# A two-layer cross-attention block on one core: the softmax maximum joined across key quarters on VectorE instead of TensorE, with edits to the seams between stages, the division and the opening

## What is computed

```python
# x (8, 56, 256), ctx (8, 1500, 256); H = 16 heads, K = 128, F = 1024; two layers, one MLP
def _cross_attention(q_in, kv_in, wq, bq, wk, bk, wv, bv, wo, bo, bias_k, bias_v):
    qh = (q_in @ wq + bq).reshape(b, q_len, H, K)
    kh = (kv_in @ wk + bk).reshape(b, t, H, K)
    vh = (kv_in @ wv + bv).reshape(b, t, H, K)
    kh, vh = concatenate([kh, bias_k]), concatenate([vh, bias_v])      # one extra key
    weights = softmax(einsum('bqhk,bthk->bhqt', qh, kh) / sqrt(K))
    return einsum('bhqt,bthk->bqhk', weights, vh).reshape(b, q_len, H * K) @ wo + bo
...
x = x + _cross_attention(layer_norm(x), ctx, ...)      # twice
return x + gelu(layer_norm(x) @ w_fc1 + b_fc1) @ w_fc2 + b_fc2
```

## Time and profile before

| | us |
|---|---|
| median of 3 runs | 1236.87 (1236.75 to 1239.4) |
| the profiled execution's own time | 1234.94 |
| its span, first to last instruction | 1233.1 |
| PE busy | 1210.1, 98% |
| PE weight load busy | 1111.1, 90% |
| POOL busy | 894.0, 72% |
| DVE busy | 833.2, 68% |
| ACT busy | 767.9, 62% |
| DMA | 68 GB/s on average |

### The profile page before, as it was taken

How to read it: one execution, slowest core, us unless ns; L and a number is a source line. 1 busy time by engine, 2 the same in 40 slices (tenths; PEclk the granted TensorE clock), 3 DMA queues, 4 the chain that set the end, 5 groups by cost and what they waited for, 6 DMA issues and landing times. The chain is left out here.

```text
span 1233.1 us, 26572 instructions
## 1 busy us (share of the span) xinstructions
PE 1210.1 (98%) x7736; PEld 1111.1 (90%) x7736; DVE 833.2 (68%) x1395; ACT 767.9 (62%) x1495; POOL 894.0 (72%) x744
## 2 busy tenths in 40 slices
PE   7999999999999999999999999999999999999998
PEld 6779999999999999998896999999999999999897
DVE  6765767676767676676755666676766666677654
ACT  5746666565666565676484656666666666667655
POOL 5737777777777787679551768686868686867882
PEclk9999999999999999999999999999999999999999
DMA  5401222222222222223320122222222222312231
GB/s 179 126 19 51 56 76 55 74 57 73 61 69 64 67 68 61 59 62 102 103 69 18 38 56 71 61 73 58 74 57 74 58 76 56 79 42 65 73 93 38
DMA packets 147720, 83.60 MB, mean 68 GB/s; under 512 B 121116, under 2 KB 122540, under 8 KB 147672
## 3 DMA queue, kind: packets, MB, share of 16 engines
q1 hardware_dynamic: 147128, 82.27, 25.5%
q10 hardware_dynamic: 544, 0.75, 0.2%
HBM read 68.56 MB, written 0.53 MB: 56 GB/s over the span
## 5 line engine op out<-in xcount | busy, mean ns | idle before, releaser
L607 POOL TENSOR_TENSOR pt<-slots,pt 125x512 fp32r<-125x512 f32 (+3 forms) x384 | 451.0, 1181 | 174.9 <-ACT slots L1069 167.6
L782 PE MATMUL psum<-qs,ctx 128*125 128x384 f32 (+1 forms) x2304 | 537.9, 370 | 3.0 <-ACT slots L1095 2.3
L782 PEld LDWEIGHTS psum<-qs,ctx 128*125 128x125 f32 x2304 | 394.2, 186 | 50.3 <-ACT slots L1095 10.1
L799 PE MATMUL psum<-ctx,pt 125*128 125x258 f32 (+1 forms) x1344 | 382.8, 285 | 1.4 <-ACT on L1076 0.5
L800 PE MATMUL psum<-ctx,pt 125*128 125x256 f32 (+1 forms) x1344 | 379.4, 282 | 0.0
L801 PE MATMUL psum<-ctx,pt 125*128 125x258 f32 (+1 forms) x1344 | 378.9, 282 | 0.0
L1068 ACT ACTIVATE pt<-slots 125x512 fp32r<-125x512 f32 (+3 forms) x384 | 221.3, 576 | 232.9 <-DVE slots L1356 221.9
L1368 DVE TENSOR_TENSOR t_max<-psum,t_max 125x512 f32<-125x512 f32 (+1 forms) x320 | 199.0, 622 | 200.9 <-PE psum L782 200.8
L1095 ACT ACTIVATE slots<-psum 125x512 f32<-125x512 f32 (+1 forms) x384 | 206.5, 538 | 121.7 <-DVE t_max L1368 112.6
L799 PEld LDWEIGHTS psum<-ctx,pt 125*128 125x128 f32 (+1 forms) x1344 | 253.5, 189 | 16.1 <-ACT on L1076 3.5
L800 PEld LDWEIGHTS psum<-ctx,pt 125*128 125x128 f32 (+1 forms) x1344 | 254.2, 189 | 6.7
(11 more groups left out here) (105 smaller groups left out, 972.4 us busy)
## 6 DMA issues: line engine op xcount, KB each, us to landing
nat_stage<-ctx_nat SPq DMA_DIRECT2D x60, 375.0 KB
tr_stage<-ctx_tr SPq DMA_DIRECT2D x60, 375.0 KB, 3.1
w_raw<-weights SPq DMA_DIRECT2D x70, 256.0 KB, 2.7
qt<-turn SPq DMA_DIRECT2D x256, 32.0 KB, 2.0
qt<-turn SPq DMA_DIRECT2D x224, 24.0 KB, 1.9
dk_rest<-dk_rows SPq DMA_DIRECT2D x2, 768.0 KB, 5.7
w_raw<-weights ACTq DMA_DIRECT2D x2, 256.0 KB, 4.6
dk_first<-dk_rows SPq DMA_DIRECT2D x2, 256.0 KB, 4.7
```

The source lines that it names most:

```text
L607: nc.gpsimd.tensor_tensor(split_weights(h, LO, c), logits(h, c), as_f32(split_weights(h, HI, c)), ALU.subtract).then_inc(pt_lo, 1)
L782: last = mm(scores(h, k), ctx_tr_chunk(half, a, c), qs[h][:, m, half, 0:R], start=(half, a, m) == terms[0], stop=(half, a, m) == terms[-1])
L799: mm(out_bank[:, 0:D + 2], hi, ctx_nat_hi(c), start=(c == 0), stop=False, skip_group_check=True)
```

## The change

1. Maximum. PE's two transposes and their waits go. DVE copies the quarters 1 to 3 of `mx_part` (32 partitions by 16 or 12 numbers) beside quarter 0, right after `turned_max`; in the next step it reduces the four (32 partitions, 64 or 48 numbers), and copies the result to partitions 32, 64 and 96. `spread_max` then reads SBUF instead of PSUM.
2. Division. ACT starts on `rden_ready` instead of `pn_ready`. The scaled tiles are two columns wider, and `pn_extra` is copied out of them later (`extra_weights`, before `turn_context`, and once at the end of a layer).
3. Seams. In `norm` the rows 1 and 3 go to ACT (`norm_rows`), rows 0 and 2 stay on DVE; one more short operation makes ACT's bias. ACT's copies of the rows to `xres` come after `norm`. The fourth key-bias product of the next layer moves into the wait for POOL's power. The mask goes on `dv80` (80x128) instead of `p80` (80x448), four buffers deep, and the first heads' mask products no longer wait for `p80`. The MLP's first two blocks use the interleaved order of the first queries.
4. Opening. `hdiff` comes after the statistics, the key-bias products of heads 0 and 1 after the first two `query_lo`, the fourth weight's high part into the query loop. Throughout the query loop a weight's high part is made one head later in ACT's order, before the copies of the carried queries.
5. `NAT_STEPS` 13 becomes 14 (DVE and POOL).

```diff
-NAT_STEPS = (9, 13, 17, 21)
+NAT_STEPS = (9, 14, 17, 21)
@@ POOL, output stage
+                def mask_values(h, u):
+                    nc.gpsimd.tensor_tensor(dvm[u][:], as_f32(dv80[:]), mask[:, ds(h, 1)].to_broadcast([EXTRA, K]),
+                                            ALU.mult).then_inc(dvm_ready, 1)
+                weight_lo(l * JOBS + H, 0)
+                for u in range(4):
+                    mask_values(u, u)
+                weight_lo(l * JOBS + (H + 1), 1)
...
                 with pool.Fori(0, QUADS - 1) as quad:
                     for u in range(4):
                         weight_lo(l * JOBS + quad * 4 + (H + 4 + u), u)
-                        mask_extra(quad * 4 + (u + 4), u % 2, l * H + quad * 4 + (u + 3))
+                        pool.wait_ge(c_mm, INIT + l * H + quad * 4 + (u + 1))
+                        mask_values(quad * 4 + (u + 4), u)
@@ PE, first_contexts
-                for u in range(2):
-                    pe.wait_ge(pm_ready, INIT + n + u + 1)
-                    mm(C_BANK[u][:, 0:ROWS], dv80[:], pm[u][:], start=False, stop=True).then_inc(c_mm, 1)
+                    pe.wait_ge(dvm_ready, INIT + n + u + 1)
+                    if u == 0:
+                        pe.wait_ge(p80_lo, INIT + n // H + 1)
+                    mm(C_BANK[u][:, 0:ROWS], dvm[u][:], p80[:], start=False, stop=True).then_inc(c_mm, 1)
@@ PE, batch_steps
-                        if c == 0 and (h == 1 or not first) and k < NCT + (0 if tail else 1):
-                            pe.wait_ge(mt_reduced, INIT + group)
-                            max_by_block(1 - h)
-                        if c == 1 and (h == 1 or not first) and k < NCT + (0 if tail else 2):
-                            pe.wait_ge(max_ready, INIT + group)
-                            max_by_query(1 - h)
@@ ACT
+            def norm_rows(m):
+                act.wait_ge(ln_chain, INIT + m * LN_CHAIN + LN_CHAIN)
+                for g in range(1, RG, 2):
+                    go(xn[:, g, :], Y_BANK[g][0:RGP, 0:D] if m else xres[:, g, :], ACT.Identity,
+                       bias=ln_b[:, g:g + 1], scale=ln_r[:, g:g + 1]).then_inc(xn_act, 1)
...
-                    act.wait_ge(pn_ready, INIT + l * GROUPS + b * 2 + (h + 1))
+                    act.wait_ge(rden_ready, INIT + l * GROUPS + b * 2 + (h + 1))
@@ DVE
+                def gathered_max(b, h):
+                    dve.wait_ge(mt_reduced, INIT + group + 1)
+                    for a in range(1, BLOCKS):
+                        V.tensor_copy(mx_part[0:BLOCK, a, 0:n], mx_part[a * BLOCK:(a + 1) * BLOCK, 0, 0:n]).then_inc(mt_gathered, 1)
                 def group_max(b, h):
-                    dve.wait_ge(mt_mm, INIT + group + 1)
-                    V.tensor_reduce(mx_group[0:n].rearrange("p (a q) -> p a q", a=BLOCKS), ...
+                    dve.wait_ge(mt_gathered, INIT + (group + 1) * (BLOCKS - 1))
+                    V.tensor_reduce(mx_all[0:BLOCK, 0:n], mx_part[0:BLOCK, :, 0:n].rearrange("p a j -> p j a"),
+                                    X, ALU.max).then_inc(max_ready, 1)
+                    dve.wait_ge(max_ready, INIT + group + 1)
+                    for a in range(1, BLOCKS):
+                        V.tensor_copy(mx_all[a * BLOCK:(a + 1) * BLOCK, 0:n], mx_all[0:BLOCK, 0:n]).then_inc(max_spread, 1)
...
-                    V.tensor_tensor(pn_extra[:, at], sums[:, D + 1], rden[:, at], ALU.mult).then_inc(pn_ready, 1)
+                def extra_weights(b, h):
+                    dve.wait_ge(on_act, INIT + l * (2 * GROUPS) + b * 4 + (2 * h + 2))
+                    dve.wait_ge(on_dve, INIT + l * (3 * B) + b * 3 + (2 + h))
+                    V.tensor_copy(pn_extra[:, tiles_of(batch_at(l, b), h)], on[:, 0:GT[h], D + 1]).then_inc(pn_ready, 1)
@@ DVE, batch_steps
                         if c == 1 and ended:
                             group_max(*ended)
                         if (i >= 0 or not first) and not (tail and i >= 0):
                             shifted(b, i, ph, pc)
                         if c >= 1 and not tail:
                             chunk_max(b, k, h, c)
                         if c == 0 and ended:
                             turned_max(*ended)
+                            gathered_max(*ended)
                         if c == 1 and ended:
                             spread_max(*ended)
```

More of the change, by code:

```diff
@@ L171, in build @@
         cs = [sb(f"cs{u}", [P, 2, ROWS], F32R) for u in range(4)]
-        pm = [sb(f"pm{s}", [EXTRA, ROWS], F32R) for s in range(2)]
+        dvm = [sb(f"dvm{u}", [EXTRA, K], F32R) for u in range(4)]
         dv80 = sb("dv80", [EXTRA, K], F32R)
@@ L655, in _ @@
                 pool.wait_ge(dv80_step, INIT + l * 2 + 2)
-                for u in range(2):
-                    weight_lo(l * JOBS + (H + u), u)
[L658 to L675, removed]
+                def mask_values(h, u):
+                    nc.gpsimd.tensor_tensor(dvm[u][:], as_f32(dv80[:]), mask[:, ds(h, 1)].to_broadcast([EXTRA, K]),
+                                            ALU.mult).then_inc(dvm_ready, 1)
+                pool.wait_ge(consts_in, 16 * N_CONSTS)
+                weight_lo(l * JOBS + H, 0)
+                for u in range(4):
+                    mask_values(u, u)
+                weight_lo(l * JOBS + (H + 1), 1)
+                pool.wait_ge(oth_lo, INIT + l * H + 2)
+                for u in range(2, 4):
+                    weight_lo(l * JOBS + (H + u), u)
                 with pool.Fori(0, QUADS - 1) as quad:
@@ L730, in first_queries @@
                         if c == DC - 1:
-                            last.then_inc(q_mm, 1)
+                            last.then_inc(done, 1)
             def residual(m):
@@ L987, in _ @@
                 keep_busy(4)
-            for u in range(2):
-                head_context(u, LAYERS * H + u, LAYERS * JOBS + u, False)
+            pe.wait_ge(c_lo, INIT + LAYERS * H - 2)
+            first_blocks(LAYERS, LAYERS * JOBS, C_BANK, c_mm)
             output_quad(LAYERS * H, LAYERS * JOBS, False, True, False)
@@ L1020, in _ @@
             go(act_ready[:], filler[:, 0:1], ACT.Copy)
-            for u in range(4):
+            for u in range(3):
                 act.wait_ge(w_in[u], 16)
@@ L1319, in query_quad @@
                             tr_part_hi(quad, quad)
-                if l == 0:
-                    dve.wait_ge(dk_first_in, 16)
-                    for u in range(2):
-                        key_bias_product(l, u, u, 0, True)
                 query_lo(0, 0)
@@ L1327, in _ @@
                 if l == 0:
-                    for u in range(2, 4):
+                    dve.wait_ge(dk_first_in, 16)
+                    for u in range(4):
                         key_bias_product(l, u, u, 0, True)
@@ L1469, in _ @@
                 normalized(B - 1, 1, O_LAST)
+                extra_weights(B - 1, 1)
                 dve.wait_ge(ot_mm, INIT + (l + 1) * 2)
```

109 lines of the change are left out of this document (56 added, 53 removed).

## The result

The changed kernel takes 1247.51 us (median of 5 runs, 1244.44 to 1247.82), the kernel before beside it 1236.87 (5 runs): a ratio of 1.0074, with a 95% interval of 1.0061 to 1.0087. The forecast was 1222.5.

What follows compares the result with a forecast made beforehand. PE's own order was taken to bound the attention loop. Loop -4.1, partial entries -2.0, attention's end -2.8, clock -1.7, seam -1.7, third norm -0.3, masks -0.5, opening -1.2: sum -14.3, so 1222.5 us, range 1206 to 1232.

Steps and rivals of the forecast that it cites:

- Copies blocked by POOL: The maximum's DVE copies within SBUF wait for a running POOL instruction: 0.15 us each unhindered, up to 1.3 blocked.
- The pair at k = 0: Transposes in steps 1 and 2 of an entry: removing them wins 0.42 us per entry.
- a race won: At k = 12, third copy against POOL's L558: won, net 0 per entry; lost, 0.45 us more; +0.22 taken.
- Part 5: `NAT_STEPS` 13 to 14 moves L1235's 0.94 us on DVE out of crowded k = 13; no term of its own.
- The division: ACT starts earlier on the scaled tiles: -0.24 us at k = 5, +0.15 at k = 17, per entry.
- First and emptying entries: Four partial entries, first and emptying of each layer: -1 us per layer, -2.0 in all.
- End of attention: First mask product no longer waits for POOL's mask: 1.4 us earlier per layer, -2.8 in all.
- Clock and output stages: Half-speed clock behind attention's end, layer 2 only: -1.7 us; shorter masks on POOL in the output stage: -0.5.
- Seam of the layers: Between layers, fourth key-bias product and its reduce moved away: 0.9 us; norm rows split between engines: 0.8; together -1.7.
- The opening: PE's 1.37 us wait for `qh` goes and the norm is earlier, but the first weight buffer is freed later: -1.2 us.
- rival (c): In the loop, spreading copies each meet one more POOL instruction: 2.3 us per entry, time 1254; chance 0.09.
- Rival (a): In the loop, the maximum's copies are not blocked: an entry wins 1.31 us, time 1208; chance 0.22.

Runs made afterwards that it cites:

- reductions and 13: Changed kernel with the six copies of each group written as maxima over an axis of one element and `NAT_STEPS` back at 13: 1213.38 us.
- experiment 1: `NAT_STEPS` step moved alone: changed kernel with 13 again, 1230.24 us; kernel before with 14, 1246.99 us.
- experiment 3: Both with 13: kernel before with the maximum joined by DVE's copies, 1243.15 us; changed kernel with the transposes on PE, 1225.92 us.
- experiment 5: On reductions and 13: `hdiff` and products back, `pn_extra` copy as a reduction, 1211.41 us; POOL's order at attention's end changed on top, 1211.00.
- experiment 4: Opening edits undone in changed kernel: 1247.01 us; `hdiff` or products alone put back in reductions and 13: 1212.38, 1213.81; opening edits alone on kernel before: 1238.00.
- part 1 alone: Kernel before with only the maximum joined by DVE's copies, no transposes on PE, `NAT_STEPS` with 13: 1243.15 us, ratio 1.0043.

## Why the prediction was wrong, step by step

- **What bounds the kernel: right.** What an entry gained or lost is PE's waits and the two pairs of transposes, and the step bases read from the earlier trace rows held: with reductions and 13 an entry is nothing but these.
- **Copies blocked by POOL: right,** and the schedule of k = 12 to 0.1 us. The pair at k = 0 won 0.39 of its 0.42 (2.84 + 2.87 for the earlier trace rows's 6.10). Steps 12 to 15 grew by 0.21 in the changed kernel, for 0.22 forecast, and that this agrees is luck: 0.22 was the middle between a race won (0) and a race lost (0.45). The race was won in all 12 middle entries (3.27 or 3.28 us each), and 0.13 at step 14 and 0.1 at step 15 were lost even so.
- **Part 5, `NAT_STEPS`, counted at nothing: this is the step that failed.** The prediction moved L1235's 0.94 us on DVE and stopped there. Behind the cast hang POOL's low part, a load on SP's queue, and DVE's own wait for it three steps later. It is +0.69 per entry by itself (experiment 1) and +1.15 in the changed kernel: 16 us, the whole distance from gain to loss. All it needed was to follow one piece round in the trace of before: cast, low part, issue, landing. There the round took 8.2 us and DVE waited 0.20 at its end; over the whole kernel with 13 it waited for that transfer only 6.9 us, but 19 times and up to 0.6: there was hardly any slack to give away.
- **The same number had hidden the cost of the copies.** With the cast at k = 13 the copies cost 0.42 per entry (experiment 3), where the two pairs were to win 0.20: DVE's cast then stands behind the blocked copies and steps 14 to 16 wait. The sum of the pairs holds only for the kernel with 14.
- **The division: mis-sized on the safe side.** k = 5 won 0.22 to 0.25 in layer 1 and 0.27 to 0.30 in layer 2 (0.24 forecast). At k = 17 the step is 2.49 in every kernel with the changed division but those with the copies and 14 together, a gain of 0.14 and not a loss of 0.15; with these it was 2.66, a loss of 0.03.
- **First and emptying entries: -2.0 forecast, +2.2 measured.** Emptying takes 24.59 and 24.58 for 24.04 and 24.06. In the changed kernel it is 24.0 with the transposes and 23.7 with reductions: leaving the transposes out is worth 0.3 and not 1, and the blocked copies cost 0.9. The first entries gained nothing, and in about half the layers they lost 1.0 to 1.2 (last section).
- **End of attention: -2.8 forecast, -1.2 measured.** POOL is out of the product's way, as said, but its second weight had moved to where it blocks DVE's low part of head 1 (experiment 5): 1.10 of DVE's chain. The prediction named that weight as late, not as something that DVE would meet.
- **Clock and output stages: -2.2 forecast, -3.1 measured.** The stretch at half clock of the earlier trace rows is gone: 1.00 throughout in all 20 stages of the ten kernels with the changed masks. With before's masks it stood in five of eight stages, in layer 1 as well as in layer 2. Layer 1's stage took 44.7 twice without it and 45.9 and 46.0 with it, so it cost 1.2 to 1.3, where I had 1.7. At full clock the changed masks still win 0.9 in layer 1 (44.70 to 43.81), where I had 0.25. Layer 2's stage at full clock, seen once (the kernel before with 14), took 45.56, 1.9 above the changed kernel's 43.66; 1.15 of it is a wait of PE for a low part of DVE's, L1479, which took 2.48 there for 1.22 beside POOL's long mask products. The masks were not changed alone, so that these gains are theirs is argued, not shown.
- **Seam of the layers: -1.7 forecast; -1.6 measured** (7.17 to 5.57); the norm before the MLP -0.6 with -0.3 in the MLP, for -0.3.
- **The opening: -1.2 forecast, 0 by time** (experiment 4).

Put together with the traces' own sizes over the whole loop: 14 for 13 +15.7, the copies +2.3, the division -4.5, so +13.5; first and emptying entries +2.2; end of attention -1.2; output stages -3.1; norms, queries and MLP -3.1: +8.3 without the opening, where the medians say +10.6. The opening's later first score chunk could be the 2.3 that are left, but by time it was worth 0 to 0.5 (experiment 4), and the executions of one kernel lie up to 5 us apart: this part stays open. The rival (c), slower by blocked spreading copies, gave the right sign for a reason that the trace denies: the copies behind a reduce lost what the forecast had, so its sign was right by luck. Rival (a), free copies, had 1.31 per entry; with reductions and 13 it is 60.88 - 59.59 = 1.29, and the time is 3 to 5 us above its 1208. By the sizes above, the emptying (1.3), the opening (1.2) and the end of attention (1.6) make up most of that in the kernel with reductions and 13; no run takes them apart.

## What to carry to other kernels

When a step is moved, follow its buffer once round (last reader, issue, landing, next reader) and hold the sum against the distance to the next use; the engine time of the step itself is the least of it. An engine that runs in order and waits for a DMA stops everything behind it, so that wait is costed by what stands behind. And where DVE moves a few numbers within SBUF beside a busy POOL, try a reduction over an axis of one element in place of a copy.

## What the runs showed of the hardware

- A DVE instruction with two tensors in SBUF is held by POOL too: L1482 took 1.37 us for 0.27, ending 0.13 after POOL's weight. The Trainium skill says so, page "SBUF — State Buffer", section "SBUF: two separate sides": two SBUF inputs take the lock as the two-port mode does. The trace agrees. I had used only its half on copies, and so misread the fourth product of the earlier trace rows. It is not long just for reading two tensors in SBUF, since the third took 0.41; it took 1.26 beside a weight instruction of POOL. The third product and POOL in the kernel before:

```profile
601.77 0.41 DVE L1271 TENSOR_TENSOR g_prod<-w_raw,dk_first 128x256 f32<-128x256 f32 x1
...
602.24 1.29 POOL L534 TENSOR_TENSOR w<-w_raw,w 128x512 fp32r<-128x512 f32 x1 [1.72 <-ACT w L1003]
```

- The cast from `nat_stage`, SBUF to SBUF, took 0.93 to 0.96 each time in every kernel, beside POOL or not. The Trainium skill, page "VectorE: DVE Perf Modes", section "What auto-detection actually checks", wants outermost dimensions on both sides that are even or equal; here it is one run of 768 against three blocks of 256. The trace fits; it wasn't tried apart.
- In the first entry of a layer, where PE waits at k = 14 and 15, the granted clock fell from 1.00 (2.4 GHz) to 0.50 (1.2 GHz) in some executions. Windows of the changed kernel with 13, layer 1, columns as in the earlier trace rows:

```profile
84.00:86.00 2.00, 1.31 (x6) 0.99 (x6) 1.87 (x4) 1.04 (x3) 0.00 (x0) 1.00 0.00 0
86.00:88.00 2.00, 1.06 (x3) 1.06 (x4) 1.45 (x3) 2.00 (x5) 1.29 (x1) 0.72 0.00 0
88.00:90.00 2.00, 2.00 (x8) 2.00 (x8) 0.74 (x2) 1.49 (x4) 1.85 (x2) 0.50 0.00 1
90.00:92.00 2.00, 2.00 (x16) 2.00 (x15) 1.54 (x3) 1.87 (x4) 1.87 (x2) 0.92 0.02 4
```

PE was busy for 2.4 of the 4 us from 84 on, and the clock then stood at 0.50 for about three: that entry took 45.88 for 44.73. It is so in 8 of 18 layers of the changed kernel and its variants with the maximum on DVE, in none of 8 with the transposes on PE, and in neither layer of part 1 alone. Steps 14 and 15 took the same 2.24 to 2.29 and 2.49 where it fell and where it did not. What decides it was not tried.
